# A vision tower with 34 experts on one core: the down product with stationary weights, the low halves of the weights on VectorE

## What is computed

```python
out = softmax((q @ k.T + mask) * inv_scale) @ v            # 16 heads, per image
h = h + out
scores = sigmoid(x @ gate_w.T)                             # x = layernorm(h), 32 experts
combine = weights of the 8 best experts of a token, taken from the 4 best of 8 groups
g = silu(einsum('th,eih->tei', x, w_gate)); u = einsum('th,eih->tei', x, w_up)
routed = einsum('tei,ehi->th', g * u * combine[:, :, None], w_down)
shared = (silu(x @ sh_gate.T) * (x @ sh_up.T)) @ sh_down.T  # 256 wide: two more experts of 128
h = h + routed + shared
```

## Time and profile before

| | |
|---|---|
| median of 3 runs | 971.75 us (969.69 to 975.0) |
| profiled execution | 968.11 us, span 966.4 us |
| PE busy | 794.9 us, 82% |
| DVE busy | 639.6 us, 66% |
| ACT busy | 420.4 us, 44% |
| POOL busy | 241.1 us, 25% |
| chain that ended last, by engine | PE 63%, DVE 19%, ACT 8% |
| attention units, about | 518 to 589 us |
| expert stage, first turns to end | 619 to 966 us |

### The profile page before, as it was taken

How to read it: one execution, slowest core, us unless ns; L and a number is a source line. 1 busy time by engine, 2 the same in 40 slices (tenths; PEclk the granted TensorE clock), 3 DMA queues, 4 the chain that set the end, 5 groups by cost and what they waited for, 6 DMA issues and landing times.

```text
span 966.4 us, 19178 instructions
## 1 busy us (share of the span) xinstructions
PE 794.9 (82%) x7446; PEld 602.6 (62%) x7446; DVE 639.6 (66%) x922; ACT 420.4 (44%) x590; POOL 241.1 (25%) x218
## 2 busy tenths in 40 slices
PE   2854964897998876976598898579999999999996
PEld 1642743794544454755277786357777777888885
DVE  3594599467878567788767786657777754545444
ACT  6243662752023332565357772445555532232222
POOL 6000497000689931000301330013333300000000
PEclk9986897979999988897999556779999999999999
DMA  7000000002000000001121110024444421222221
GB/s 282 1 1 1 3 1 1 3 2 87 0 1 0 1 1 1 1 1 35 34 40 43 51 52 1 1 77 144 143 145 144 130 71 53 63 66 71 63 63 50
DMA packets 24355, 46.59 MB, mean 48 GB/s; under 512 B 2637, under 2 KB 10573, under 8 KB 23917
## 3 DMA queue, kind: packets, MB, share of 16 engines
q1 hardware_dynamic: 24301, 45.82, 15.2%
HBM read 42.51 MB, written 1.36 MB: 45 GB/s over the span
## 4 chain that ended last, share of the span: by engine, by line
PE 63%; DVE 19%; ACT 8%; issue 6%; POOL 3%; DMA 1%; DVEq 0%; POOLq 0%; ACTq 0%
PE psum L1666 10%; PE psum L1667 10%; PE psum L1668 10%; PE psum L1822 6%; PE psum L791 4%; PE psum L1832 4%; PE psum L792 4%; PE psum L793 4%; ACT arena L1088 3%; PE psum L1950 1%; DVE arena L1355 1%; PE psum L1802 1%; PE psum L1872 1%; ACT arena L1202 1%; DVE arena L1538 1%
## 5 line engine op out<-in xcount | busy, mean ns | idle before, releaser
L1666 PE MATMUL psum<-xh,arena 128*128 128x296 f16 (+1 forms) x664 | 195.8, 295 | 13.8 <-issue 4.9
L1667 PE MATMUL psum<-xl,arena 128*128 128x296 f16 (+1 forms) x664 | 195.9, 295 | 0.0
L1668 PE MATMUL psum<-xh,arena 128*128 128x296 f16 (+1 forms) x664 | 195.6, 295 | 0.0
L791 PE MATMUL psum<-arena 128*128 (+3 forms) x340 | 93.4, 275 | 6.0 <-DVE arena L659 6.0
L714 DVE TENSOR_TENSOR arena<-psum,arena 128x592 f32<-128x592 f32 x64 | 49.6, 775 | 67.6 <-PE psum L1668 58.3
L792 PE MATMUL psum<-arena 128*128 (+3 forms) x340 | 93.5, 275 | 0.0
L793 PE MATMUL psum<-arena 128*128 (+3 forms) x340 | 93.3, 274 | 0.0
L618 ACT ACTIVATE arena<-arena 128x592 f16<-128x592 f32 x68 | 47.4, 697 | 105.1 <-DVE arena L653 104.1
L659 DVE TENSOR_TENSOR arena<-arena 128x592 f16<-128x592 f32 x68 | 52.7, 775 | 59.0 <-ACT arena L618 58.9
L1666 PE MATMUL psum<-arena 128*74 128x74 f16 (+3 forms) x348 | 61.0, 237 | 33.1 <-POOL arena L913 18.0
L1666 PEld LDWEIGHTS psum<-xh,arena 128*128 (+2 forms) x664 | 66.1, 100 | 35.1 <-issue 15.3
(11 more groups left out here) (321 smaller groups left out, 1706.1 us busy)
## 6 DMA issues: line engine op xcount, KB each, us to landing
arena<-comb SPq DMA_DIRECT2D x64, 296.0 KB, 3.3
arena<-in_wmoe SPq DMA_DIRECT2D x34, 384.0 KB, 3.0
arena<-in_xt SPq DMA_DIRECT2D x4, 864.0 KB, 9.4
arena<-in_w SPq DMA_DIRECT2D x2, 1024.0 KB, 5.8
arena<-arena SPq DMA_DIRECT2D x6, 187.0 KB
arena<-in_ctrl SPq DMA_DIRECT2D x1, 1056.0 KB, 9.1
out<-arena SPq DMA_DIRECT2D x2, 512.0 KB, 3.1
arena<-in_wlin SPq DMA_DIRECT2D x1, 768.0 KB, 4.5
```

Source lines behind the costliest of these rows:

```text
L791: pe.matmul(dst, hi, W[:, i, s_, 0, 2 * D:3 * D], start=start and t % 2 == 0, stop=False, skip_group_check=True)
L1666: pe.matmul(dst, wh, mh, start=start, stop=False)
L1667: pe.matmul(dst, wh, ml, start=False, stop=False)
L1668: return pe.matmul(dst, wl, mh, start=False, stop=stop)
```

## The change

- `down` is turned round: the weights (2 blocks of 128 output features) are stationary and the activations move, 296 columns at a time. So 4 accumulators (2 feature blocks x 2 token chunks) x 3 matmuls, with features on the partitions, in banks 0, 1, 2 and 7. Bank 7 is also the router's, so in the first pass the fourth part of `down(0)` stands behind the transposes of the combine weights.
- The residual transposes ahead of the experts and their copies to `htok` are gone. At the end of a pass DVE adds the four accumulators into `hT` (4 operations of 296 columns), PE transposes this half of `hT` (10 transposes, in groups of 4, 4 and 2), and ACT copies the 3 groups to `res`. For the first pass this stands behind the first `gate_up` of the second pass.
- The low half is one DVE operation for all experts (`weight_low`). ACT's scaling in place and POOL's subtraction are gone. In the first pass's loop it stands at the end of DVE's turn.
- `LEAD` is 4. In the attention, high halves are made at the units 3, 5, 9 and 11, low halves at 5 and 7 (of the first two experts). The low halves of the other two are made in ln4, ahead of the reciprocal (`meanwhile`). Experts 4 and 5 have their high halves between the first two turns and their low halves behind the router's chain.

```diff
-LEAD = 6
+LEAD = 4
...
-LOW_AT = [3, 5, 7, 9, 11, 13]
+HIGH_AT = [3, 5, 9, 11]
+LOW_AT = [5, 7]
...
-        GATE_UP, ACC = 3, 0
+        GATE_UP, ACC = 3, (0, 1, 2, 7)
...
-        def moe_pool(pool):
-            def low(i, s_):
-                return pool.tensor_tensor(W[:, i, s_, 1], wraw[:, s_], W[:, i, s_, 0], ALU.subtract)
...
+        def weight_low(dve, i, s_, count):
+
+            dve.wait_ge(ev["whi"], count)
+            dve.scalar_tensor_tensor(W[:, i, s_, 1], wraw[:, s_], WS, W[:, i, s_, 0], ALU.mult, ALU.subtract).then_inc(
+                ev["wlo"], 1)
...
             act.activation(W[:, i, s_, 0], wraw[:, s_], ACT.Copy, scale=WS).then_inc(ev["whi"], 1)
-            act.activation(wraw[:, s_], wraw[:, s_], ACT.Copy, scale=WS).then_inc(ev["wsc"], 1)
...
+            def rows_out(hf):
+                if hf:
+                    act.wait_ge(ev["stored"], 32)
+                for n in range(3):
+                    act.wait_ge(ev["outT"], 3 * hf + n + 1)
+                    w, m = (2, 128) if n < 2 else (1, HALF - 512)
+                    act.activation(res[0:m, 2 * n:2 * n + w], banks[ACC[n]][0:m, 0:w * D].rearrange(
+                        "p (i d) -> p i d", d=D), ACT.Copy).then_inc(ev["res"], 1)
...
+                    with dve.Fori(1, first) as i:
+                        for s_ in range(2):
+                            turn(i * 2, s_, i * 16)
+                            weight_low(dve, i + LEAD // 2, s_, i * 2 + (LEAD + s_ + 1))
...
+                for x in range(4):
+                    c, ch = x % 2, x // 2
+                    if x == 0:
+                        dve.wait_ge(ev["down0"], hf + 1)
+                    elif x == 2:
+                        dve.wait_ge(ev["dn"], NX * (hf + 1))
+                    tokens = hT[:, c, hf * HALF + CH * ch:hf * HALF + CH * ch + CH]
+                    dve.scalar_tensor_tensor(tokens, psum[:, ACC[x], 0:CH], 1.0 / (AS * WS), tokens, ALU.mult,
+                                             ALU.add).then_inc(ev["summed"], 1)
...
-                    pe.matmul(dst, hi, W[:, i, s_, 0, 2 * D:3 * D], start=start and t % 2 == 0, stop=False, skip_group_check=True)
-                    pe.matmul(dst, hi, W[:, i, s_, 1, 2 * D:3 * D], start=False, stop=False, skip_group_check=True)
-                    ins = pe.matmul(dst, lo, W[:, i, s_, 0, 2 * D:3 * D], start=False, stop=stop, skip_group_check=True)
...
+                    high, low = (W[:, i, s_, kind, 2 * D + 128 * c:2 * D + 128 * c + 128] for kind in range(2))
+                    pe.matmul(dst, high, ah[:, s_, cols(ch)], start=start, stop=False, skip_group_check=True)
+                    pe.matmul(dst, high, al[:, s_, cols(ch)], start=False, stop=False, skip_group_check=True)
+                    ins = pe.matmul(dst, low, ah[:, s_, cols(ch)], start=False, stop=stop, skip_group_check=True)
...
+            def rows_out(hf):
+                for n in range(3):
+                    pe.wait_ge(ev["summed"], 4 * hf + (2, 4, 4)[n])
+                    for t, _, m in half_tiles(0)[2 * n:2 * n + 2]:
...
+                if hf:
+                    rows_out(0)
                 gate_up(hf, 0, 1, base, False)
...
-            norm("ln4", lead=turned_back)
+            def last_lows():
+                for e in range(len(LOW_AT), LEAD):
+                    weight_low(dve, e // 2, e % 2, e + 1)
+
+            norm("ln4", lead=turned_back, meanwhile=last_lows)
```

More of the change, by code:

```diff
@@ L79 @@
     + ["att_s", "att_max", "att_e", "att_p", "att_hi", "att_lo", "att_t", "att_pa", "att_pb", "att_o", "att_n"]
-    + ["combine", "whi", "wsc", "wlo", "gu", "silu", "t1", "a", "ah", "al", "dn", "res"]
+    + ["combine", "whi", "wlo", "gu", "silu", "t1", "a", "ah", "al", "dn", "down0", "summed", "outT", "res"]
 )
@@ L167, in plan_tiles @@
     add(("lg",), "act")
-    for n in range(5):
-        add(("hR", n), "act")
     for n in range(3):
@@ L263, in tower @@
         banks = [psum[:, i] for i in range(8)]
-        router_bank = {("lg",): 7, **{("hR", n): n % 3 for n in range(5)}, **{("cT", n): 7 for n in range(3)}}
+        router_bank = {("lg",): 7, **{("cT", n): 7 for n in range(3)}}
         n0 = place[("f2", 0, 0)][0]
@@ L451, in tower @@
         al = carve(31200, 2, HALF, dt=F16)
-        htok = carve(31792, NT, D)
         LG = 34352
@@ L596, in moe_act @@
             after(act, ("lg",))
[L597 to L606, removed]
             def turn(e2, s_, first, loop):
@@ L708, in moe_dve @@
             rest(0, 1, True)
+            for x in range(2):
+                weight_low(dve, LEAD // 2, x, LEAD + x + 1)
             def turn(e2, s_, count):
@@ L749, in moe_pe @@
             ins.then_inc(filled[who(("lg",))], 1)
-            for n in range(5):
-                if n >= 3:
-                    after(pe, ("hR", n - 3))
-                bk = bank(("hR", n))
-                for ti in (2 * n, 2 * n + 1):
-                    _, t0, m = half_tiles(ti // HT)[ti % HT]
-                    for c in range(2):
-                        at = (ti % 2) * D + 128 * c
-                        ins = pe.transpose(bk[0:m, at:at + 128], hT[:, c, t0:t0 + m], ident[:])
-                ins.then_inc(filled[who(("hR", n))], 1)
             def combine_rows():
@@ L798, in moe_pe @@
                 gate_up(hf, 0, 0, base, hf == 0)
+                if hf:
+                    rows_out(0)
                 gate_up(hf, 0, 1, base, False)
                 if hf:
[L801 to L805 removed]
+                    pe.wait_ge(ev["res"], 3)
+                    down(0, 0, base, start=True)
+                else:
+                    down(0, 0, base, start=True, parts=range(3))
                     combine_rows()
+                    after(pe, ("cT", 2))
+                    down(0, 0, base, start=True, parts=(3,))
                 with pe.Fori(1, NX // 2) as i:
                     gate_up(hf, i, 0, i * 2 + base, False)
[L809 removed]
+                    down(i - 1, 1, i * 2 + (base - 2))
                     gate_up(hf, i, 1, i * 2 + base, False)
[L811 to L812 removed]
+                    down(i, 0, i * 2 + base)
+                down(NX // 2 - 1, 1, base + NX - 2, stop=True)
+            rows_out(1)
         @block.sync
```

69 lines of the change are left out of this document (30 added, 39 removed).

## The result

The changed kernel takes 958.44 us (median of 4 runs, 952.57 to 959.32) where the kernel before took 972.25 beside it: a ratio of 0.985 [0.983, 0.988], which is 12.0 to 16.6 us less. The forecast was 956.0, with 950 to 964 as its range.

What follows compares the result with a forecast made beforehand. It took DVE's chain, held up by POOL, to bound the first pass, PE the second, and PE at 1.2 GHz the attention. Terms -5.1 - 6.2 - 4.9 + 0.5 = -15.7 us gave 956.0, range 950 to 964.

Steps and rivals of the forecast that it cites:

- The loop: Experts' loop: 26 first-pass turns from 4.77 to 4.53 us, -6.2; 38 other turns 0.13 shorter each, -4.9 us.
- rival 1: First pass: low half near 1.40 us makes DVE the bound, turn 4.8, 963.7 us in all; chance 0.12.
- The attention: Fewer low halves, earlier high halves: the stall and the longer pairs shrink, together -5.1 us.
- The first gap: Attention: of PE's 3.03 us stand until 536.18, behind DVE's wait for ACT's high half, 2.8 us gained.
- The pairs: Attention: 5 longer pairs of units lose their excess of 4.34 over 3.87 us, -2.35 us.
- Rival 2: Attention gains little because ACT's queue sets the pace and the stall moves to it: about 961 us; chance 0.08.
- ln4: Two low halves ahead of the reciprocal, 2.0 us, fit in DVE's 2.89 us wait there: cost 0.
- Router's stage: No gain from the transposes and copies that leave; 0, or up to 0.6 us lost if PE's clock falls.
- Second pass's start: Ten transposes, 0.83 us, fill PE's 0.96 us gap between the first two gate_up: cost 0, at worst 1.0.
- End: After the last matmul, sums, transposes, copies and hand-overs take 2.7 us against 2.22: +0.5, up to 1.3.
- Rival 3: Attention at the full clock: 12 units at about 2.9 us instead of 3.87, 944 us in all; chance 0.06.
- Rival 4: First pass's loop slower than before because raw weight slots load later and landings are long: 992 us; chance 0.02.

Runs made afterwards that it cites:

- e9: Kernel after, plus one unused DVE operation of 384 columns behind each low half in the first pass's loop; 957.04 us in one run.
- e2: Kernel after, but in the first pass's loop ACT scales the raw weights and POOL makes the low halves again; 961.16 us, ratio 0.9904.
- e4: Kernel after, plus an unused 16-bit POOL subtraction beside each low half in the first pass's loop; 988.02 us in one run.
- e1: Kernel after with the attention's part undone: six experts split ahead, halves behind the old units; 964.97 us, ratio 0.9935.
- e5: Kernel after, plus one unused DVE operation of 96 columns ahead of each low half in the loop; 954.12 us in one run.
- e6: Kernel after, plus 20 unused transposes on PE ahead of the first gate_up in the router's stage; 958.74 us, ratio 0.984.
- e3: Kernel before with its loop's low halves on DVE, without POOL and ACT's scaling, its own down kept; 968.69 us, ratio 0.9985.
- e8: Kernel after, plus 8 unused matmuls of 296 columns ahead of each attention unit's scores; 948.47 us, ratio 0.974.
- e10: Kernel after, plus 2 unused matmuls of 296 columns ahead of each attention unit's scores; 941.86 us, ratio 0.970.
- e12: Kernel before, plus 4 unused wide matmuls ahead of each attention unit's scores, its old low halves kept; 977.91 us, ratio 1.006.
- e7: Kernel after, plus 4 unused matmuls of 296 columns ahead of each attention unit's scores; 941.38 us, ratio 0.968.
- e11: Kernel after with 4 unused matmuls a unit, 20 behind the experts' first gate_up and 8 before the combine weights' wait; 942.85 us, ratio 0.972.

## Why the prediction was right, and where its steps were off

**The loop, -11.1 forecast, -10.8 measured** (-6.56 - 4.21). The turn came out at 4.53 in both passes. The low half has 0.958 us as its mean in the loop (x28) and 0.950 outside, where I took 1.0 from the size of L1355. The step that was off is DVE's own turn: 4.4 in the prediction, 4.19 by e9. The stated threshold for rival 1, a low half of 1.13 us, was therefore too low; it is 0.96 + 0.34 = 1.30. Rival 1's price at 1.40 was too high for the same reason: DVE's turn would have been 4.63, not 4.8. e2 shows the -6.2 to be POOL's (+6.34 when it comes back; e4 has the same mechanism with POOL alone).

**The attention, -5.1 forecast, -4.7 measured.** The first gap gave 2.74 (2.8 forecast). The pairs gave 1.98 (2.35 forecast): nearly all units now take 3.91 where the shorter of a pair took 3.87, which over ten units is the missing 0.35. e1 gives both back to 0.02 us. Rival 2 is thereby out.

**ln4, 0 forecast, -1.4 in this pair of profiles.** The hiding was right: the two low halves take 1.82 us and the reciprocal still waits for ACT. What I held at 0 without a reason is the clock. From the reciprocal to the sigmoid both kernels have 7.74 us of DVE, and PE takes 3.16 before and 2.58 after at granted clocks of 0.59 and 0.69, which is the whole 0.58. The stretch ahead of it (16th unit to reciprocal) has 0.68 before and 0.72 after. Every kernel here with the change's units and no fillers (after, e2, e4, e5, e6, e9) has 21.95 and 10.70 us in these two stretches, to 0.01, and those with the old units (before, e1, e3) have 22.77 and 11.28. So the -1.4 is no accident of one execution: it came along with the attention's part, and as far as the granted clocks tell by a shift of the clock's rise and fall. With fillers other pairs appear (21.95 and 11.28 in e8, e10 and e12; 20.8 and 10.9 in e7 and e11), so neither the number of experts split ahead nor the place of the low halves sets them. The prediction had named this phase and put no number on it.

**Router's stage, 0 to +0.6 forecast, +0.36 measured.** As forecast, the granted clock fell there (second and third `gate_up` partly at the low level), and PE, not the DMA, now releases the first routed `t1`. The +0.36 is luck, though. PE's wait ahead of the second `gate_up` was 3.73 us, not 5.6, as the first `gate_up` too ran at the low clock in part. What I had not priced is the third `gate_up`, which took 5.5 us (642.75 to 648.23) and so released `t1` late. And the stretch varies: it is 27.05, 27.27 and 28.08 us with the old start (e12, e3, before; granted clock 0.86, 0.86, 0.80), and 28.44, 28.50, 28.53 and 29.11 with the new one (after, e5, e9, e1; 0.70 in the first, 0.75 in the last). The middle values differ by 1.2 us, twice my 0.6. The Trainium skill (TensorE: Matmul & The Clock Gate, "Why this matters for your kernels") warns of idle gaps between bursts; the trace agrees in direction, with 0.70 in this stretch against 0.80 before. The same page's "Part 4: PE-mode transpose" says that a transpose doesn't count as busy in the same way. e6 fits that, with 0.70 in spite of 20 more of them, but it doesn't show it: the kernel before has 0.80 with 20 transposes in the same place.

**Second pass's start, 0 forecast.** Right: 1.12 us of transposes stand between two `gate_up`, in place of the gap of 0.96.

**End, +0.5 forecast, +0.34 measured.** The parts that the prediction lists for its 2.7 (1.05, 0.5, half of 0.83, 0.5) add up to 2.47, so they made +0.25.

**The sum, -15.7 forecast.** The stretches of the trace behind the first unit give -16.2, the medians -13.8 [-16.6, -12.0]. The forecast's 956.0 is 2.4 under the measured 958.44, less than the runs' own spread. The traces come that close to the sum by a cancellation: ln4's -1.4, which I had at 0, makes up for the attention, the loop and the router's stage, each 0.3 to 0.4 us dearer than forecast.

**Rival 3, the attention at the full clock: 944 forecast for that case.** It didn't come by itself, as I argued, but one half of my reason was wrong. The right half first. In the kernel before the clock doesn't fall in the wait at 532 (on PE from 533.2 to 536.2). It falls while PE works, ahead of it, as windows of that trace show, and so it fell in the kernel after too.

```profile
528.00:531.60 3.60, 2.68 (x88) 2.33 (x87) 0.82 (x2) 3.54 (x5) 1.58 (x2) 1.00 0.02 5
531.70:533.10 1.40, 1.40 (x46) 0.89 (x40) 0.46 (x1) 1.40 (x3) 1.14 (x1) 0.50 0.00 0
533.20:536.10 2.90, 0.00 (x0) 0.00 (x0) 2.87 (x5) 0.67 (x2) 0.03 (x1) 0.50 0.33 77
```

The wrong half: from 98% busy at 0.50 I concluded that the mix of these units keeps the clock low. e7 and e10 show that a small addition to the mix is enough to hold it, at 941.4 and 941.9 us. What I had not separated is holding from regaining: all that my row from 536 to 544 shows is that the clock does not come back. The units ahead of the fall are not 98% busy; they have PE waits of 0.9 to 1.1 us each at the full clock, and that part of the trace I had not weighed. e7's ratio stands 16.4 us under the kernel after's. Its trace behind the first unit is 12.6 us shorter, 12.2 of them ahead of the router's sigmoid; the rest lies within the two intervals.

**Rival 4** never showed: no low half waits for its raw weights.

## What to carry to other kernels

When two engines are within a few per cent of each other in a loop, each improvement alone shows only up to the other's bound (2.6 and 4.1 us here), and both together show more than the sum (10.4). Read an engine's own turn from one in which it waits for nothing, or lengthen it until the loop gives way (e5, e9); the distance between its starts in a loop that another engine bounds is too long. And where a stage of small matmuls runs at 1.2 GHz though PE is always busy, try two wide unused ones in each step ahead of the fall, after removing any long PE wait there. Here they gave more than the whole change did (16.4 us against 13.8), and with the wait still there they lost.

## What the runs showed of the hardware

- The low half and the product, DVE operations with both inputs in SBUF, are held up by nearly all that is left of a POOL operation on SBUF: 2.40 us against 0.95 with a 1.64 us POOL operation (e4), also when the POOL operation is 16-bit and touches none of the same buffers. It holds the other way round too: in the kernel after the POOL operation that starts at 551.94, 0.38 us behind a low half in the attention, takes 1.69 us where its like take 1.26, and that low half takes its plain 0.95. The Trainium skill (SBUF — State Buffer, "The single rule") calls the shared port pair an exclusive lock; the trace agrees.
- The granted clock can stay at 0.50 over 52 us in which PE is busy for 50.8, and at 1.00 over 41 us in which it is busy for 38.9 (95%). The busy share is not what tells them apart; what differs is two or four matmuls of 296 columns in each unit, and what went before.
- When a DVE operation doesn't read what the one before it wrote, its start can lie up to 0.08 us ahead of that one's end in the trace (0.47 for 0.56 and 0.87 for 0.95 in e9, 0.18 for 0.26 in e5). The product, which reads `t1`, starts 0.10 us behind its end (695.39 for 695.29 in e9). So a sum of lengths isn't the length of a chain; take start to start.
